# Local projections one iteration earlier, parts stored once, stack rows repeated by the loads, causal side jobs in another order

## What is computed

```python
# layer 0: 16 heads of 8; key j is seen by query i when j <= i and j >= i - 128
x = layernorm(x + softmax(mask(q @ k.T * 8 ** -0.5)) @ v @ w_out.T)
# layer 1: the same with a causal mask, on layer_norm(x); then
x_resid = h + attention(layer_norm(h)) @ w_o
xf = layer_norm(x_resid)
probs = softmax(xf @ w_gate); top_w, top_i = top_k(probs, 2)      # eight experts
out = sum_e gate_e * (gelu(xf @ w1[e] + b1[e]) @ w2[e] + b2[e])
x = layernorm(h + out + x_resid)
```

## Time and profile before

| | us |
|---|---|
| median of three runs | 867.57 |
| the profiled execution | 870.4 |
| its span | 868.6 |
| PE busy in the span | 655.7 (75%) |
| DVE | 509.7 (59%) |
| ACT | 462.6 (53%) |
| POOL | 429.8 (49%) |

### The profile page before, as it was taken

The page is one execution under the profiler, slowest core; times in us unless marked ns, Lnnn a source line. Parts: engine busy times, 40 slices in busy tenths (PEclk is TensorE's granted clock), DMA queues, the critical chain, the costliest instruction groups (busy, mean ns, idle before and its releaser), DMA issues.

```text
span 868.6 us, 19900 instructions
## 1 busy us (share of the span) xinstructions
PE 655.7 (75%) x7512; PEld 393.1 (45%) x7512; DVE 509.7 (59%) x1116; ACT 462.6 (53%) x671; POOL 429.8 (49%) x649
## 2 busy tenths in 40 slices
PE   2557978978887878888788888886614999999900
PEld 0323434434443433444343444442313998898900
DVE  1644667676776888798888879882340222222236
ACT  2035655655674565766677666666502554554503
POOL 4015556556654543245464647458640454445445
PEclk8568999998997998999999999999855999999965
DMA  5635544643643637334362707101014566566464
GB/s 170 157 90 115 138 109 100 154 126 67 159 116 46 153 97 135 102 76 135 66 159 42 185 25 190 43 16 53 20 58 161 187 204 214 184 223 213 168 163 128
DMA packets 73583, 107.45 MB, mean 124 GB/s; under 512 B 8104, under 2 KB 60048, under 8 KB 70428
## 3 DMA queue, kind: packets, MB, share of 16 engines
q1 hardware_dynamic: 68892, 97.86, 42.2%
q0 software_dynamic: 4608, 8.47, 3.3%
HBM read 44.14 MB, written 38.90 MB: 96 GB/s over the span
## 4 chain that ended last, share of the span: by engine, by line
PE 32%; DMA 22%; DVE 17%; issue 10%; SPq 7%; POOL 6%; ACT 4%; another core or an unknown queue 0%; POOLq 0%; ACTq 0%; DVEq 0%
DMA parts_dram<-parts 9%; DMA arena<-parts_dram 7%; PE pair_ps L1415 6%; PE o_ps L1278 6%; SPq L439 4%; PE o_ps L1434 3%; PE pair_ps L1299 3%; PE pair_ps L1198 3%; POOL rows_dram L628 3%; DMA rows_dram<-rows,row_at 3%; PE misc L1434 3%; DVE row_max L878 2%; ACT probs L707 2%; DVE row_max L876 2%; PE pair_ps L1258 1%
## 5 line engine op out<-in xcount | busy, mean ns | idle before, releaser
L707 ACT ACTIVATE probs<-pair_ps 128x1024 f32<-128x1024 f32 x272 | 275.4, 1022 | 116.2 <-PE pair_ps L1198 107.5
L1278 PE MATMUL o_ps<-probs,v_aug 128*32 128x256 f32 (+3 forms) x2048 | 166.0, 421 | 9.1 <-POOL probs L616 3.5
L603 POOL TENSOR_SCALAR_AFFINE_SELECT probs<-probs 128x512 f32<-128x512 f32 x96 | 61.2, 637 | 140.4 <-ACT probs L707 139.4
L1198 PE MATMUL pair_ps<-arena 50*128 50x256 bf16 (+3 forms) x1024 | 108.2, 288 | 26.6 <-DMA arena<-shift_t 6.5
L673 POOL DMA_INDIRECT outputs_dram<-o_norm,arena x80 | 77.7, 971 | 100.5 <-DVE o_norm L1128 80.0
L867 DVE TENSOR_REDUCE row_max<-pair_ps 128x4 f32<-128x768 f32 x96 | 89.7, 953 | 46.7 <-PE pair_ps L1232 46.1
L838 ACT ACTIVATE probs<-pair_ps,arena 128x256 f32<-128x256 f32 x160 | 65.4, 471 | 76.3 <-PE pair_ps L1415 66.0
L876 DVE TENSOR_REDUCE row_max<-pair_ps 128x2 f32<-128x1024 f32 x64 | 77.2, 1219 | 15.8 <-PE pair_ps L1258 14.7
L1415 PE MATMUL pair_ps<-x_t,arena 128*128 128x256 f32 x320 | 80.8, 397 | 7.1 <-DMA arena<-pack 3.9
L1198 PEld LDWEIGHTS pair_ps<-arena 50*128 50x128 bf16 x1024 | 32.7, 95 | 108.9 <-issue 45.5
L1278 PEld LDWEIGHTS o_ps<-probs,v_aug 128*32 128x32 f32 x2048 | 48.6, 111 | 66.0 <-issue 39.5
(11 more groups left out here) (147 smaller groups left out, 1107.8 us busy)
## 6 DMA issues: line engine op xcount, KB each, us to landing
arena<-pack SPq DMA_DIRECT2D x40, 578.0 KB
arena<-parts_dram SPq DMA_DIRECT2D x96, 192.0 KB
...
```

The lines of the kernel that those rows point to most:

```text
L707: nc.scalar.activation(probs[:, n % PROBS, :], pair_ps[RING_AT["score", n][0]][:, :, :].rearrange("p b t -> p (b t)"), ACT.Exp, scale=SCAL ...
L1198: last = nc.tensor.matmul(pair[:, r, col:col + width], k_st[u % STACKS][own, gs, j * P:(j + 1) * P], q_st[u % STACKS][own, gs, q0:q0 + wid ...
L1278: last = nc.tensor.matmul(o_ps[c * VHEAD:(c + 1) * VHEAD, q0:q0 + width], v_aug[u % 2][:, j, first:first + VHEAD], probs[:, slot, r * T + ...
```

## The change

It has four parts. First, `parts_dram` holds each part once, in two buffers, and a part is stored by one DMA of 256 KB with both sides. The repeats are made by the loads, which read an 8-row piece two or three times through a repeated leading dimension: four loads of the high part (3 times 8 rows each), then eight (two of 2 times 8 rows, four of 8 rows, two of 16 rows). Second, a local unit is projected at k = 8 of iteration u - 3, and its stores and loads stand in the SyncE queue behind the shift rows of that iteration; causal units stay at k = 1 of iteration u - 2. Third, unit 1's maxima all lie in iteration 0. Fourth, the causal side jobs move: moments k = 8, variances 9, root ahead of the mask of 10, `apply` 11, transpose 13, copy of the rows 13 (was 16), `top_two` ahead of the maxima, rank 19 with `place` at the start of the next iteration, sends at k = 2 to 9.

```diff
-Q_SLOTS = (slice(0, 3), slice(4, 6), slice(3, 4))
-K_SLOTS = (slice(2, 5), slice(1, 6, 4), slice(0, 1))
-HIGH_ROWS = ((0, 24), (16, 40))
-LOW_ROWS = (((24, 48),), ((0, 16), (40, 48)))
+LOW, MIDDLE, HIGH = 0, 1, 2
+FIRST_LOADS = (((0, (HIGH,), 3),), ((2, (HIGH,), 3),))
+LATER_LOADS = (((4, (MIDDLE,), 2), (3, (LOW,), 1)), ((5, (MIDDLE,), 1), (0, (LOW, MIDDLE), 1)))
...
-STACK_LOADS = 5 * TILES_R * 16
+STACK_LOADS = 6 * TILES_R * 16
...
     for u in range(UNITS):
         slots = []
-        if u - 2 >= -1:
+        if u - 2 >= 0:
...
-    CAUSAL: {0: ("xt",), 2: ("v",), 5: ("on",), 7: ("out",), 14: ("xf",), 15: ("shift",), 16: ("logits",), 18: ("rank",)},
+    CAUSAL: {0: ("xt",), 2: ("v",), 5: ("on",), 7: ("out",), 13: ("xf",), 15: ("shift",), 16: ("logits",), 19: ("rank",)},
...
-    if it < 0:
-        return k if it == -2 and 0 <= k < 2 else None
-    return it + 2 if real(it + 2) and k == (0 if layer(it + 2) == LOCAL else 1) else None
+    if it == -2:
+        return k if 0 <= k < 2 else None
+    if k == 8 and real(it + 3) and layer(it + 3) == LOCAL:
+        return it + 3
+    return it + 2 if k == 1 and real(it + 2) and layer(it + 2) == CAUSAL else None
...
+def jobs_before(it, k):
+
+    if k:
+        return jobs_at(it, k - 1)
+    return jobs_at(it - 1, steps(it - 1) - 1) if it > -2 else []
...
-        scratch = nc.dram_tensor("parts_dram", (2, SLOTS, P, T), BF16, kind="Internal").ap()
+        scratch = nc.dram_tensor("parts_dram", (2, 2, PARTS, P, T), BF16, kind="Internal").ap()
...
                 def store(part, ready):
                     sp.wait_ge(ready, u + 1)
-                    for side, slots in ((0, Q_SLOTS), (1, K_SLOTS)):
-                        place = scratch[side, slots[part]].rearrange("s p t -> p s t")
-                        sp.dma_start(place, parts[:, part, side, :].unsqueeze(1).to_broadcast(place.shape)
-                                     ).then_inc(stored_low if part else stored_high, 16)
-
-                def load(side, first, last):
-                    stack = (q_st, k_st)[side][u % STACKS]
-                    by_row = scratch[side].rearrange("s (d r g) t -> (s d) r (g t)", d=HD, r=TILES_R)
-                    for r in range(TILES_R):
-                        sp.dma_start(stack[HALF * r + first:HALF * r + last, :, :].rearrange("p g t -> p (g t)"), by_row[first:last, r, :]
-                                     ).then_inc(stack_in[u % STACKS], 16)
-
-                if u:
-                    sp.wait_ge(stack_in[(u - 1) % STACKS], ((u - 1) // STACKS + 1) * STACK_LOADS)
-                store(0, high_ready)
-                store(1, middle_ready)
+                    sp.dma_start(scratch[u % 2, :, part].rearrange("s p t -> p s t"), parts[:, part, :, :]).then_inc(stored[part], 16)
+
+                def load(pieces_of):
+                    for side, stack in ((0, q_st), (1, k_st)):
+                        for slot, which, times in pieces_of[side]:
+                            count = len(which)
+                            source = scratch[u % 2, side, which[0]:which[0] + count].rearrange("s (d r g) t -> (s d) r (g t)", d=HD, r=TILES_R)
+                            for r in range(TILES_R):
+                                first = HALF * r + HD * slot
+                                place = stack[u % STACKS][first:first + HD * times * count, :, :].rearrange("p g t -> p (g t)")
+                                rows_of = source[:, r, :] if times == 1 else source[:, r, :].unsqueeze(0).to_broadcast([times, HD, GS * T])
+                                sp.dma_start(place, rows_of).then_inc(stack_in[u % STACKS], 16)
+
+                if u >= 2:
+                    sp.wait_ge(stack_in[(u - 2) % STACKS], ((u - 2) // STACKS + 1) * STACK_LOADS)
+                store(HIGH, high_ready)
+                store(MIDDLE, middle_ready)
                 if u >= STACKS:
                     sp.wait_ge(score_filled, BEFORE[u - STACKS + 1])
-                sp.wait_ge(stored_high, (u + 1) * 32)
-                for side in range(2):
-                    load(side, *HIGH_ROWS[side])
-                store(2, low_ready)
-                sp.wait_ge(stored_low, (u + 1) * 64)
-                for side in range(2):
-                    for rows_of_part in LOW_ROWS[side]:
-                        load(side, *rows_of_part)
+                sp.wait_ge(stored[HIGH], (u + 1) * 16)
+                load(FIRST_LOADS)
+                store(LOW, low_ready)
+                sp.wait_ge(stored[MIDDLE], (u + 1) * 16)
+                sp.wait_ge(stored[LOW], (u + 1) * 16)
+                load(LATER_LOADS)
...
-                if it >= 0 and real(it + 2):
+                if it >= 0 and real(it + 2) and layer(it + 2) == CAUSAL:
                     load_stacks(it + 2)
...
                 if real(it + 1):
                     load_shift(it + 1)
+                if it >= -1 and real(it + 3) and layer(it + 3) == LOCAL:
+                    load_stacks(it + 3)
...
                 for k in range(steps(it)):
+                    if real(w) and k == 10:
+                        root(w)
                     if real(it):
                         mask(it, k)
-                    if real(w) and k == 10:
-                        root(w)
                     if real(w) and layer(w) == CAUSAL and k == 12:
                         add_residual(w)
-                    if real(it - 2) and layer(it - 2) == CAUSAL and k < CHOICES:
-                        send(it - 2 - B, k)
+                    if real(it - 2) and layer(it - 2) == CAUSAL and 2 <= k < 2 + CHOICES:
+                        send(it - 2 - B, k - 2)
...
-                    if real(w) and layer(w) == CAUSAL and k == 16:
+                    if real(w) and layer(w) == CAUSAL and k == 13:
                         copy_rows(w)
...
-                    before = dict(jobs_at(it, k - 1))
+                    before = dict(jobs_before(it, k))
+                    if "logits" in before:
+                        top_two(before["logits"])
...
                     if real(w):
+                        if k == 8:
+                            moments(w)
                         if k == 9:
-                            moments(w)
-                        if k == 10:
                             variances(w)
-                        if k == 12:
+                        if k == 11:
                             apply(w)
-                    if "logits" in before:
-                        top_two(before["logits"])
...
+            place(UNITS - 1)
             plan()
```

20 lines of the change are left out of this document (10 added, 10 removed).

## The result

Both kernels on one chip: 868.01 us before (867.06 to 868.99), **1045.99 us** after (1041.92 to 1050.01), a ratio of 1.205, interval 1.200 to 1.211. Slower, as forecast, but above the range: 972 was forecast, with 1040 as its upper end. The profiled execution of the changed kernel has a span of 1048.2 us, against 868.6 before. A second measurement on another chip gave a ratio of 1.200 (1.192 to 1.208). Ratios are taken over the undisturbed runs of both kernels, so they can differ a little from the quotient of two medians.

The account below looks back on a forecast made before the run. No engine fills the time; the longest link is waiting for a unit's stack loads. Start +23.2, iterations 0 to 4 +40.5, 5 +1.9, 6 and 7 +16, 8 to 13 +22.6: 867.6 + 104.2 = 972 us, range 910 to 1040.

Parts of the forecast that it names:

- (b): A unit's later loads: 22 rows on the first engine for 8, +2 us (+0 to +4.5), 11.4 us to landing.
- (e): Local loop from projection to projection through SyncE's queue: 39.7 us an iteration; first term, projection to shift load, 9.5 us.
- causal sum: Iterations 8 to 13: longer waits for the stack, then later normalisation behind the row sends, less 0.5 an iteration: +22.6 us.
- (a): A unit's first loads: busiest engines carry 32 rows for 8, +7.7 us; first to later loads 14.0 us.
- (c): A unit's high store: one DMA of 256 KB for two of 384 KB, 3.2 us for 3.9, between 0 and -1.2.
- (f): Causal side jobs moved: -0.5 us an iteration (0 to -1.5), but three steps of slack between sends and normalisation go.
- "hidden" rival: Loads narrow, but hidden in the causal half, where sends get through: causal -4 for +22.6, 922 us; chance 0.25.
- fast rival: Loads with repeated rows spread over 12 and 16 engines like plain ones: loop 27.5 us, total 839 us; chance 0.12.

Follow-up runs that it names:

- e9: The kernel before, with only a unit's four first loads reading their source by a repeat of three (3 x 8 rows): ratio 1.120.
- e10: The kernel before, with only the q side's 24 rows of the later loads cut into 8 rows and 2 x 8 by a repeated source: ratio 1.055.
- e1: The changed kernel, two buffers kept, with stores writing the repeats again and ten plain loads reading them: 894.58 us, ratio 1.047.

## Why the prediction was right and wrong

**What missed.** The time came out 75.4 us above the forecast's +104.2: 38.3 of them in iterations 8 to 13, 23.0 in iterations 0 to 4, 3.7 at the start, 2.4 in iterations 6 and 7, and 8.0 in the other columns. The steps that failed are (b), the later loads' term, the first term of (e), and above all the causal sum, which let the row sends and not the stack set iterations 10 to 13.

**Right: the direction and its mechanism.** A load whose source is read with a repeat in front uses 3 engines, not 12: share 0.20 in the changed kernel and in e9, and three tiny packets a load in the changed kernel. The Trainium skill's rule on the engine count (DMA: Bandwidth & Descriptors, "Why a DMA increments its semaphore by 16 and not by 1") agrees with it, now for a repeated source as well. Later loads stood 13.2 to 14.1 us behind the first ones in the local units for a predicted 14.0, so (a) held, and with it 0.32 us a row (0.33). From the high store to the first loads it is 2.2 to 2.8 us for a predicted 3.2. First score 81.61 for 77.9, start +26.9 for +23.2. TensorE waits at every local projection for x_t, and in iteration 5 for the stack, 6.2 us for 7. Iterations 6 and 7: +18.4 for +16. Right, too, that the loop from projection to projection sets iterations 0 to 4.

**Wrong (b), the later loads.** "I take +2", with a bound of +4.5: by the trace 14.7 us from the first later issue at 229.51 to the projection at 244.17, for a predicted 11.7, and 14.5 to the causal stack, for 11.4. So the term was +5, above its bound. What failed is the overlap: the prediction saw that 8 rows explain only 2.6 of the 9.4 us of before, and let most of the 14 extra rows of the first two engines pass in the rest. The later portion in the changed kernel, then in the kernel before:

```profile
229.50:232.50 3.00, 3.00 (x56) 1.46 (x55) 1.70 (x2) 2.54 (x3) 2.13 (x4) 1.00 0.19 38
232.50:238.50 6.00, 2.16 (x40) 1.42 (x38) 3.02 (x11) 1.02 (x1) 2.33 (x4) 0.93 0.95 144
239.50:244.00 4.50, 0.00 (x0) 0.00 (x0) 0.00 (x0) 0.00 (x0) 0.00 (x0) 0.50 0.12 48
```

```profile
196.40:198.00 1.60, 1.60 (x33) 0.56 (x25) 1.22 (x2) 1.48 (x2) 0.98 (x1) 1.00 0.26 77
198.00:204.00 6.00, 5.61 (x112) 3.44 (x108) 4.73 (x13) 3.65 (x6) 4.48 (x9) 1.00 0.97 153
```

All sixteen engines are at work for about 6 us in both, at 9 to 10 GB/s each, 0.8 to 0.9 us a row. In the changed kernel this starts 3.0 us after the first issue instead of 1.6, and behind it two engines work alone until 244, at 24 GB/s each, 0.34 us a row: 14 rows of that are 4.8 us. So there was no room for the extra rows; they stand behind the others nearly in full. The causal unit has the same end (share 0.15 from 556 to 560.5), and so has e10, which has only this portion changed and lost 5.5%. The row that could have warned is the earlier trace rows itself: 87 GB/s at a share of 0.53 is 10 GB/s an engine, against 22 for the ones loads. The prediction worked out that 0.8 us and set it aside as what 16 engines do together; but that is the state in which the later loads begin, and the 9.4 us are filled by it.

**Wrong (e), the loop's first term.** From the projection to the shift load 11.8 us for 9.5. The projection's own loss at the low clock was in, at 1.2 us; it took 3.78 us for 2.0. That the steps after it run at the low clock too was not in, nor that the second of them waits for VectorE's step behind the projection:

```profile
200.80:204.60 3.80, 3.76 (x6) 1.23 (x8) 0.00 (x0) 0.00 (x0) 0.00 (x0) 0.50 0.00 1
204.60:208.50 3.90, 3.06 (x49) 1.79 (x48) 2.79 (x3) 3.84 (x5) 1.22 (x2) 0.50 0.00 0
...
207.00 0.61 PE L1208 MATMUL pair_ps<-arena 50*128 50x256 bf16 x4 [0.84 <-DVE rest L908]
```

Behind 9.1 us without work the granted clock is 0.50, 1.2 GHz, up to 208.5, and a score takes 0.61 us for 0.39. The row that the prediction took its 1.2 us from, 150.71, is no such case: TensorE had been idle for 0.58 us only, and the clock was 1.00 until then (147.0 to 150.7). The mean granted clock over the loop from 200.8 to 244.2 is 0.78, over an iteration of before 0.89. Together with (b), less 0.8 each for (a) and (c): 43.4 for 39.7. The other loops were longer still: the four from 109.91 to 287.70 average 44.4, 19 us more than four of 39.7, and the first of them began 4.7 us late.

The windows (us, busy time of each engine, clock, DMA share, GB/s) of a local loop of the changed kernel, and of a stretch behind a wait for the stack in its iteration 10:

```profile
200.80:244.20 43.40, 29.99 (x413) 14.82 (x413) 23.22 (x37) 18.39 (x21) 18.35 (x27) 0.78 0.28 68
560.80:576.40 15.60, 13.02 (x147) 6.29 (x147) 10.96 (x36) 7.87 (x13) 2.98 (x7) 0.85 0.02 6
```

**Wrong (f) and the causal sum, the largest miss: +60.9 for +22.6.** The prediction let the sends, not the stack, set iterations 10 to 13, at 5.5 us each. In the changed kernel the normalisation waits for them 0.38, 0.53, 0 and 0.98 us in these iterations (its longest wait, 7.1 us, comes in iteration 15); the first:

```profile
547.86 3.81 DVE L983 TENSOR_SCALAR rows<-y,mean_var,rstd 128x128 f32<-128x128 f32 x4 [0.38 <-DMA rows_dram<-rows,row_at]
```

Its last send is issued at 545.36 and has landed by 547.8, at a DMA share of 0.27 (537 to 548); in e1 the last send, issued at 474.22, takes 5.8 us, at a share of 0.86 (470 to 480). So the sum took a cost that belongs to loads on all engines, and left out most of the one that belongs to loads on three. TensorE's projection, the maxima that need the stack, and the next projection, first before (iteration 11), then in the changed kernel (iteration 10; the maxima at 560.79 are above):

```profile
436.98 1.96 PE L1299 MATMUL pair_ps<-x_t,weights 128*128 128x512 f32 x4
...
463.97 0.25 PE L1252 MATMUL pair_ps<-first_b,eye_b 64*128 64x128 bf16 x4
...
477.11 1.96 PE L1299 MATMUL pair_ps<-x_t,weights 128*128 128x512 f32 x4
```

```profile
525.92 1.98 PE L1309 MATMUL pair_ps<-x_t,weights 128*128 128x512 f32 x4
...
576.42 1.98 PE L1309 MATMUL pair_ps<-x_t,weights 128*128 128x512 f32 x4
```

The stack is there 34.9 us after the projection for a predicted 31.7, of which (b) is 3.1; it is needed at 27.0, not 27.6. That is 7.9 us where the step had 4.1. And behind the wait of 6.1 us the iteration runs at a lower granted clock, 0.85 for 1.00 in the same stretch of before (464.0 to 477.1): 15.6 us to the next projection for 13.1, a term that the causal sum had nowhere. That is 10.4 us an iteration; measured are 11 to 13 in each of iterations 10 to 13, where 5.5 were forecast, and 4.4 and 9.5 in 8 and 9. The sends did get through, as the "hidden" rival had it; but the stack did not come in time, and that rival, which let the causal half gain, is ruled out with it.

**The fast rival would have failed too.** 839 us was to come out if the loads spread. e1 comes close to that kernel (it stores the repeats, the rival did not): 1.047 of before. Its loop was 31.6 us, not 27.5 (the prediction's own terms, 8.3 + 1.3 + 3.2 + 6.3 + 9.4, make 28.5), and (f) struck there.
